# Gated cross-attention block: softmax totals summed across partitions by ScalarE copies, K jobs halved

## The reference

```python
q = (layernorm(x) @ Wq).reshape(b, t, 32, 128); k = (ctx @ Wk).reshape(b, t, 8, 128); v = (ctx @ Wv)
q, k = apply_rope(q), apply_rope(k)
logits = 30 * tanh(einsum('btkgd,bTkd->bkgtT', q, k) * 0.0884 / 30)
weights = softmax(where(mask, logits, -1e30), axis=-1)
x = x + tanh(g_xattn[0]) * (einsum('bkgtT,bTkd->btkgd', weights, v).reshape(b, t, 4096) @ Wo)
gate, up = layernorm(x) @ Wg, layernorm(x) @ Wu            # dequantised weights
x = x + tanh(g_ffn[0]) * ((gate * sigmoid(gate) * up) @ Wd)
```

## Time and profile before

| | us |
|---|---|
| median of 3 runs | 789.41 (788.84 to 790.84) |
| the profiled execution | 787.43 |
| its span, first to last instruction | 785.6 |
| TensorE busy | 733.1 |
| VectorE busy | 609.8 |
| ScalarE busy | 428.7 |
| GpSimd busy | 504.6 |

### The profile page before, as it was taken

One profiled execution on the slowest core, in us unless ns is written; L12 is line 12 of the kernel. 1 busy time (PEld: TensorE's weight loads), 2 busy tenths in 40 slices (PEclk: granted clock), 3 DMA queues, 4 the chain that ended last, 5 costly groups with the idle time before them and its releaser, 6 DMA issues. The chain is left out here.

```text
span 785.6 us, 11042 instructions
## 1 busy us (share of the span) xinstructions
PE 733.1 (93%) x3394; PEld 605.7 (77%) x3394; DVE 609.8 (78%) x930; ACT 428.7 (55%) x772; POOL 504.6 (64%) x377
## 2 busy tenths in 40 slices
PE   3768999999999999999999999999778689999998
PEld 3657788888888888888888888888656568888786
DVE  6658979879797887979889887988877588788521
ACT  4446666656565665565666656665453344555520
POOL 5428677776677777757786775776686456656400
PEclk9989999999999999999999999999898799999999
DMA  9500102200200210030020002002220234442011
GB/s 275 149 13 15 42 16 66 67 1 14 94 15 28 92 30 0 15 104 5 27 99 23 1 28 95 0 1 65 64 64 0 53 88 98 103 108 46 1 68 40
DMA packets 70621, 41.53 MB, mean 53 GB/s; under 512 B 23242, under 2 KB 63050, under 8 KB 70570
## 3 DMA queue, kind: packets, MB, share of 16 engines
q1 hardware_dynamic: 70570, 40.90, 18.6%
HBM read 38.77 MB, written 2.11 MB: 52 GB/s over the span
## 5 line engine op out<-in xcount | busy, mean ns | idle before, releaser
L567 POOL TENSOR_TENSOR aT_lo<-attn,aT_hi 128x512 fp32r<-128x512 f32 x64 | 83.1, 1299 | 96.0 <-ACT aT_hi L758 96.0
L501 POOL TENSOR_TENSOR q_sin<-q_sin,q_tab 128x512 f32<-128x512 f32 x64 | 82.7, 1293 | 41.4 <-ACT q_sin L659 38.7
L55 PE MATMUL ps_o<-wo_hi,aT_hi 128*128 128x512 f32 x256 | 102.6, 401 | 4.7 <-POOL acc L573 3.5
L55 PE MATMUL bank_q<-xT_hi,wq_hi 128*128 128x512 f32 x256 | 101.1, 395 | 3.2 <-issue 3.2
L57 PE MATMUL ps_o<-wo_hi,aT_lo 128*128 128x512 f32 x256 | 101.8, 398 | 0.0
L56 PE MATMUL ps_o<-wo_lo,aT_hi 128*128 128x512 f32 x256 | 101.5, 396 | 0.0
L56 PE MATMUL bank_q<-xT_lo,wq_hi 128*128 128x512 f32 x256 | 100.6, 393 | 0.0
L57 PE MATMUL bank_q<-xT_hi,wq_lo 128*128 128x512 f32 x256 | 100.4, 392 | 0.0
L666 ACT CAST qT_hi<-bank_q 128x512 fp32r<-128x512 f32 x64 | 37.5, 587 | 114.4 <-DVE bank_q L912 114.4
L493 POOL TENSOR_TENSOR probs<-probs,keepT 128x512 f32<-128x512 f32 x64 | 83.1, 1298 | 13.5 <-ACT probs L768 13.4
L904 DVE TENSOR_TENSOR bank_q<-bank_q,q_tab 128x512 f32<-128x512 f32 x64 | 44.7, 699 | 45.2 <-ACT q_sin L659 45.0
(11 more groups left out here) (214 smaller groups left out, 2074.5 us busy)
## 6 DMA issues: line engine op xcount, KB each, us to landing
wq_raw<-in_Wq SPq DMA_DIRECT2D x32, 256.0 KB, 2.8
wo_raw<-in_Wo SPq DMA_DIRECT2D x8, 1024.0 KB, 5.3
packed<-in_gate_q SPq DMA_DIRECT2D x40, 64.0 KB, 2.2
packed<-in_up_q SPq DMA_DIRECT2D x40, 64.0 KB, 2.2
packed<-in_down_q SPq DMA_DIRECT2D x10, 256.0 KB, 3.4
acc<-in_x SPq DMA_DIRECT2D x8, 256.0 KB, 5.3
cT_raw<-in_ctx SPq DMA_DIRECT2D x8, 256.0 KB, 5.7
wk_raw<-in_Wk SPq DMA_DIRECT2D x8, 256.0 KB, 2.6
```

The lines of the kernel that those rows point to most:

```text
L55: nc.tensor.matmul(out, w_hi, m_hi, start=first, stop=False)
L501: nc.gpsimd.tensor_tensor(by_seq(q_sin[:]), by_seq(q_sin[:]), q_tab[:, 1, :].unsqueeze(1).to_broadcast([P, HALF, T]), ALU.mult).then_inc(q ...
L567: nc.gpsimd.tensor_tensor(aT_lo[:], attn[:], aT_hi[:].bitcast(F32), ALU.subtract).then_inc(a_split, 1)
```

## The change

In slots 0 to 55 the fold matmul is left out. VectorE's reduce writes the first quarter of a wider `partial`; ScalarE (`cross_blocks`) copies the two halves of the partitions crosswise into the second quarter, waits for its own copies, and copies blocks of 32 partitions crosswise into the third and fourth with four more; VectorE adds the four quarters (`total`) ahead of the reciprocal. In slots 56 to 63 (`ON_PE`) the fold matmul stays. K jobs are cut in two halves of six matmuls, each in a slot of its own (`K_AT`, `K_FIRST`); V jobs are moved (`V_AT`) so that each slot has a V job or half a K job; K jobs end one slot sooner than before. The order in which weight parts are rounded and loaded is moved to suit.

```diff
-V_AT = (-5, -4, -1, 0, 1, 3, 5, 7)
+V_AT = (-6, -5, -2, 0, 2, 3, 6, 7)
+K_AT = ((-4, -3), (-1, 1), (4, 5), (8, 9))
+K_FIRST = (1, 2)
+ON_PE = TAIL
...
-            parts = {0: [("wo", g, 3)], 1: [("wv", (g + 1) // 2, 0), ("wv", (g + 1) // 2, 1)] if g % 2 else [],
-                     2: [("wq", g + 1, 0)], 3: [("wq", g + 1, 1)], 4: [("wq", g + 1, 2), ("wk", g + 1, 0)],
+            parts = {0: [("wv", (g + 1) // 2, 0), ("wv", (g + 1) // 2, 1)] if g % 2 else [], 1: [("wo", g, 3)],
+                     2: [("wk", g + 1, 0), ("wq", g + 1, 0)], 3: [("wq", g + 1, 1)], 4: [("wq", g + 1, 2)],
                      5: [("wq", g + 1, 3)], 6: [("wo", g + 1, 0), ("wo", g + 1, 1)], 7: [("wo", g + 1, 2)]}[b]
...
+        def k_parts(s):
+            return [(4 * p + i, part) for p in range(KV // 2) for i in range(4) for part in range(2)
+                    if (K_FIRST if p == 0 and i == 1 else
+                    tuple(2 * B * p + at for at in K_AT[i]))[part] == s] if s >= 0 else []
         def k_of(s):
-            return [(s + 2) // HALF] if s >= 0 and (s + 2) % HALF == 0 and (s + 2) // HALF < 2 * KV else []
+            return [kj for kj, part in k_parts(s) if part == 1]
...
                     load_wq(g, 0)
                     load_wq(g, 1)
+                    load_wk(g)
                     if g == 1:
                         store_zeros()
                     else:
                         load_wo(g)
                     load_wq(g, 2)
-                    load_wk(g)
                     load_wq(g, 3)
...
+                def cross_blocks(s):
+                    act.wait_ge(p_summed, s + 1)
+                    wait(act, quarters_summed, s)
+                    nc.scalar.copy(partial[0:64, 1, :], partial[64:P, 0, :])
+                    nc.scalar.copy(partial[64:P, 1, :], partial[0:64, 0, :]).then_inc(halves_crossed, 1)
+                    act.wait_ge(halves_crossed, s + 1)
+                    for to, of in ((0, 32), (32, 0), (64, 96), (96, 64)):
+                        cp = nc.scalar.copy(partial[to:to + 32, 2:4, :], partial[of:of + 32, 0:2, :])
+                    cp.then_inc(quarters_crossed, 1)
...
                     for kj in k_of(s - 1):
                         round_k(kj)
+                    if 0 <= s - 1 < ON_PE:
+                        cross_blocks(s - 1)
                     for n in q_of(s):
                         turn_q(n)
...
-                    dve.wait_ge(tot_done, s + 1)
                     wait(dve, norm_done, s)
-                    nc.vector.reciprocal(r_small[:], ps_tot[:, 0:GC // 32]).then_inc(inverted, 1)
+                    if s < ON_PE:
+                        dve.wait_ge(quarters_crossed, s + 1)
+                        nc.vector.reduce_sum(total[:], partial[:].rearrange("p i c -> p c i"), AX_X).then_inc(quarters_summed, 1)
+                        dve.wait_ge(quarters_summed, s + 1)
+                        nc.vector.reciprocal(r_small[:], total[:]).then_inc(inverted, 1)
+                    else:
+                        dve.wait_ge(tot_done, s - ON_PE + 1)
+                        nc.vector.reciprocal(r_small[:], ps_tot[:, 0:GC // 32]).then_inc(inverted, 1)
...
-                    pe.wait_ge(p_summed, s + 1)
-                    nc.tensor.matmul(ps_tot[:, 0:GC // 32], fold[:], partial[:], start=True, stop=True).then_inc(tot_done, 1)
+                    if s >= ON_PE:
+                        pe.wait_ge(p_summed, s + 1)
+                        nc.tensor.matmul(ps_tot[:, 0:GC // 32], fold[:], partial[:, 0, :], start=True, stop=True).then_inc(tot_done, 1)
...
-                    for kj in k_of(s):
-                        make_k(kj)
+                    for kj, part in k_parts(s):
+                        make_k(kj, (part,))
```

More of the change, by code:

```diff
@@ L142, in flamingo_block @@
         fold = sb("fold", [P, P], F32)
-        partial = sb("partial", [P, GC // 32], F32)
+        partial = sb("partial", [P, P // 32, GC // 32], F32)
         r_small = sb("r_small", [P, GC // 32], F32)
+        total = sb("total", [P, GC // 32], F32)
         live_rows = over("live_rows", [P, T], F32, wo_at[1])
@@ L229, in flamingo_block @@
         tot_done, inverted, norm_done = sem("tot_done"), sem("inverted"), sem("norm_done")
+        halves_crossed, quarters_crossed, quarters_summed = sem("halves_crossed"), sem("quarters_crossed"), sem("quarters_summed")
         p_turned, p_summed, r_spread, fold_done = sem("p_turned"), sem("p_summed"), sem("r_spread"), sem("fold_done")
@@ L1085, in sum_p @@
                     dve.wait_ge(p_turned, s + 1)
-                    wait(dve, tot_done, s)
-                    nc.vector.reduce_sum(partial[:], r_tot[:].rearrange("p (c e) -> p c e", e=32), AX_X).then_inc(p_summed, 1)
+                    wait(dve, quarters_summed, min(s, ON_PE))
+                    wait(dve, tot_done, s - ON_PE)
+                    nc.vector.reduce_sum(partial[:, 0, :], r_tot[:].rearrange("p (c e) -> p c e", e=32), AX_X).then_inc(p_summed, 1)
                 def p_rest(s):
@@ L1255, in make_q, with make_k @@
                     mm.then_inc(q_done, 1)
-                def make_k(kj):
+                def make_k(kj, parts=range(2)):
                     g, half = kj // 2, kj % 2
[L1260 to L1268, removed]
+                    if 0 in parts:
+                        pe.wait_ge(wk_split, g + 1)
+                        if g == 0:
+                            for b in range(half * HALF, (half + 1) * HALF):
+                                pe.wait_ge(ctx_lo[b], 1)
+                        wait(pe, k_split, kj)
+                    for part in parts:
+                        for k in (2 * part, 2 * part + 1):
+                            mm = split_matmul(nc, bank_kv[:], wk_hi[:, k, :], wk_lo[:, k, :],
+                                              four(cT_hi, k, half), four(cT_lo, k, half), k == 0, k == KT - 1)
+                    if 1 in parts:
+                        mm.then_inc(k_done, 1)
                 def make_v(v):
@@ L1294, in weigh @@
                     g, b = s // B, s % B
-                    if s == 0:
+                    if s == ON_PE:
                         pe.wait_ge(fold_done, 2)
```

## The result

The changed kernel takes **826.16 us** (median of 4 runs, 824.81 to 830.54) against 789.12 (787.88 to 790.84) for the kernel before beside it: a ratio of 1.0471, interval 1.0447 to 1.0496. It is slower, as forecast, but by 37 us instead of 24: the time lies 2 us above the range. The profiled execution took 825.76 us, its span is 824.0.

What follows compares the result with a forecast made beforehand. TensorE bounds at 8.48 us a slot; after the change the ScalarE-VectorE cycle does, at 8.85. 17.9 + 9.7 - 4.2 = +23.4 on 787.43 gives 810.8, plus 2.0 for the median: 813 us, range 797 to 824.

Steps and rivals of the forecast that it cites:

- the fold's 0.25 a slot: TensorE's fold matmul left out: forecast to take 0.22 us off a slot, 12.3 us over 56 slots, leaving 8.26 a slot.
- the slack: Spare time of the other engines behind TensorE in the kernel before: 1.05 us a slot, from ScalarE's waits before `turn_q` and `turn_k`.
- the cycle: ScalarE and VectorE chain `turn_q`, `cos_q`, `normalise`, `add_q`, `round_q`, next `turn_q`, closing once a slot: forecast 8.85 us, over TensorE's 8.26.
- The disputed cost: Six ScalarE copies ahead of `turn_q`: 1.45 us a slot without overlap, 0.89 with full overlap; the forecast took 1.45.
- The reduce: VectorE's added `total` between `cos_q` and `add_q`: 0.28 us a slot, between 0.21 and 0.38.
- The fixed part of the cycle: Per-slot time without extras: 1.52 + 3.46 + 0.72 = 5.70 us; with copies and reduce 7.43.
- The first slots: Slots 1 to 7, with Wk's load waiting for K job 1's second half in slot 2: forecast +9.7 us.
- The last slots: Slots 56 to 59, copies gone and K job 15 made sooner: forecast 29.3 us after 33.5, so -4.2.
- The sum: Whole kernel: 17.9 + 9.7 - 4.2 = +23.4 us, giving 810.8 profiled and 813 as median.
- the cycle loses more: Rival: copies at 0.25 and the reduce at 0.38 make 0.35 more in 54 slots, +19, 832 us; chance 0.05.

Runs made afterwards that it cites:

- the same with the two other edits: Changed kernel with normalise ahead of `cos_q`, last copy reading from partition 0, K job 1 whole in slot 2 and Wk rounded in slot 3: 782.90 us, ratio 0.990.

## Why the prediction was right and where it failed

**What held.** TensorE bounded the kernel before with about a microsecond of slack behind it (the moved schedule alone, the extra copies and normalise ahead in the kernel before all say so); the change takes the fold's 0.25 a slot (forecast 0.22) off TensorE and puts more than the slack on the cycle, which becomes the bound (no wait left before `turn_q`, TensorE's holes at `ps_pv`). The disputed cost, copies that do not overlap, was taken from the right row: 1.48 measured, 1.45 forecast. The reduce is 0.29, forecast 0.28.

**The fixed part of the cycle.** The first failed step. I took 1.52 for the three rounding issues from the earlier trace rows, where ScalarE's last SBUF read had started on partition 0. The copies change what that read is. `round_a` is held for 0.13, in a place six to nine instructions behind the last copy, where I did not look for a cost of theirs. 48 x 0.13 = 6.2 of the 7.5 us by which slots 8 to 55 were too short; undoing it alone gave back 5.7. The rest, 0.03 a slot, is about the copies' own difference (1.48 for 1.45). I had used the rule "no overlap when the start partition changes" only between neighbours.

**The first slots.** The second failed step. I saw that Wk's load would wait for the second half of K job 1, and priced it from TensorE's work alone: `k_done` at 69.7, Wk there at 72.4. I did not ask what the first half of that job, now a slot earlier, reads. It needs the last context parts, made at 64 to 65 us; hence the hole of 4.36, slower matmuls behind it, and Wk rounded at 78.39. Counted from `add_q` of slot 0 that made slot 2 end 5.0 us later than forecast; 2.2 came back, since the three zero steps in slot 3 took 0.87 instead of the 3.2 of the earlier trace rows, which the forecast had moved over unchanged, and slots 4 to 7 added 0.6. Three runs bear the cause out: with the K work moved later the first slots fell from 74.1 to 70.7 (and a wait for Wk's rest took the place); with normalise ahead they fell from 72.4 to 66.1 by the same move (together with the copies' new order) and to 62.1 with the K work as late as before.

**The last slots.** -1.9 instead of -4.2. Slot 59 took 8.38 where I had 6.4. The steps of the second layer norm stand ahead of normalise in VectorE's slot, and the first of them waits for GpSimd:

```profile
594.32 0.69 DVE L1087 BATCH_NORM_STATS2 stats<-acc 128x6 f32<-128x512 f32 x1 [0.47 <-POOL acc L584]
...
595.35 0.26 DVE L1130 RECIPROCAL r_small<-ps_tot 128x16 f32<-128x16 f32 x1
```

From the wait to normalise's reciprocal that is 1.5 us (593.85 to 595.35). I priced the slot by TensorE's Q job, 6.4, and left VectorE's extra steps out. This is read from the trace; no run changed it.

**The sum.** 7.5 + 3.4 + 2.3 from these three, +1.1 ahead of slot 0 (ten of the profiled executions spread over 57.5 to 59.5 there) and +0.7 after slot 59, not looked into: 15.0, which is 825.76 - 810.8. All five errors point the same way, and the range had none of them in it: its ends came from the sizes of the copies and the reduce, which were the best known terms. The rival "the cycle loses more" had the right side and the wrong reason; copies of 0.25 and a reduce of 0.38 do not occur.

**What I did not see.** That the cycle was long by choice of order. `normalise` stood between `cos_q` and `add_q` though VectorE waits for `turn_q` ahead of `cos_q` for 62.8 us in slots 8 to 55 of the changed kernel. With it moved, and the first slots mended, the same change is a gain.

## What to carry to other kernels

When work moves off a bounding engine, write out the cycle of the next one and the place of each instruction in it: what counts is not an engine's busy share but what stands between a release and the wait that it ends, and an instruction that fits in an engine's own wait is free. Price a new instruction also by what it does to the first later instruction that touches the same memory, and a job that is moved earlier by everything that it reads. Try the parts alone before dropping the whole: here one part lost, one gave nothing alone and 6 us later, and the gain appeared only when a third thing was moved.

## What the runs showed of the hardware

- ScalarE's hold reaches over instructions on the other memory: `round_a` at 0.61 or 0.48 after `round_q`, depending on the partition on which the last SBUF read, six to nine instructions earlier, had started (64 or 0; 96 holds it as well).
- The length of a small ScalarE copy hardly depends on its columns: 0.20 for 16, 0.22 for 32. The step from one to the next is 0.12 on the same partitions and 0.21 to 0.24 when the start changes.
- The same three VectorE steps on 192 integers took 0.35, 0.26 and 0.26 where GpSimd stood idle, and in the kernel before 0.70, 1.24 and 1.26 where GpSimd was busy. VectorE and GpSimd after, then GpSimd before:

```profile
86.85 0.35 DVE L1064 TENSOR_TENSOR zero_nibs<-zero_words,nib 128x192 uint32<-128x192 uint32 x1
87.24 0.26 DVE L1069 TENSOR_SCALAR zero_nibs<-zero_nibs 128x192 uint32<-128x192 uint32 x1
87.53 0.26 DVE L1071 CAST zero_bytes<-zero_nibs 128x192 uint8<-128x192 uint32 x1
...
88.28 1.27 POOL L578 TENSOR_TENSOR aT_lo<-attn,aT_hi 128x512 fp32r<-128x512 f32 x1 [1.98 <-ACT aT_hi L780]
...
75.08 1.42 POOL L493 TENSOR_TENSOR probs<-probs,keepT 128x512 f32<-128x512 f32 x1
76.49 1.29 POOL L567 TENSOR_TENSOR aT_lo<-attn,aT_hi 128x512 fp32r<-128x512 f32 x1
```

  GpSimd is idle from 86.30 to 88.28 after, and busy from 75.08 to 77.78 before. No run was made to change this alone, but all fourteen traces sort by it: of the second and third of these steps, the 17 that begin while GpSimd is idle last 0.26, and the 11 that begin while it runs an instruction last 1.20 to 1.33. One execution has one of each (three extra copies, 78.08 and 78.37: 0.26 and 1.27, with GpSimd idle until 78.23). The Trainium skill, GPSIMD Engine Reference, section "Specifications", says that GpSimd shares its SBUF interfaces with VectorE and that they contend for some kinds of VectorE instruction; these rows agree, and here it makes a step of 0.26 up to five times as long.
- The changed kernel and the one with only normalise ahead have the same instructions up to slot 0, yet `add_q` of slot 0 stands at 58.97 in the one profile and at 63.17 in the other. Busy table from 54 to 58 us of the changed kernel, then of the one with normalise ahead:

```profile
54.00:58.00 4.00, 4.00 (x25) 3.54 (x24) 2.59 (x5) 3.83 (x8) 0.44 (x1) 1.00 0.17 49
...
54.00:58.00 4.00, 2.98 (x7) 2.43 (x8) 2.92 (x7) 2.53 (x6) 0.33 (x1) 0.50 0.00 2
```

  The granted clock is 1.00 in the first and 0.50, the lower of its two levels, in the second, during the Q job for which slot 0 waits. Of the fourteen profiled executions, ten have this `add_q` at 57.5 to 59.5 and four (normalise ahead in the changed kernel, the same with the two other edits, normalise ahead in the kernel before, and six extra copies) at 62.3 to 63.9. The granted clock from 54 to 58 us is 1.00 in all of the ten and 0.50 to 0.60 in the four. What makes it stay low there in some executions is open; it goes with an `add_q` that is 4 to 5 us later and blurs comparisons of a few us.
